# A Mamba scan taken in pairs of channel chunks, with the sum over states done by accumulating transposes

## Chip, cores and metric

One Trainium2 chip, one of its cores. The metric is the time of the whole kernel on the device in microseconds, the median of three runs. The kernel computes two transformer-like layers, and the change touches one helper that runs three times in it.

## The reference, cut to what matters

Each of the two layers adds an attention over a long context, a Mamba block and a feed-forward block to `x` (16 x 64 tokens of 512 channels). The Mamba blocks come down to a recurrence over the 64 tokens of each sequence, for each channel d and each of 16 states n:

```
xp = einsum('bld,rd->blr', x, x_proj_w)          # gives dt_in, B, C
dt = softplus(dt_in @ dt_proj_w + dt_proj_b)
dA = exp(dt[..., None] * A)                       # decay
dBx = dt[..., None] * B[:, :, None, :] * x[..., None]
h = dA_t * h + dBx_t                              # over tokens
y = einsum('bdn,bn->bd', h, C_t)                  # sum over the 16 states
y = y + D * x                                     # the skip
```

The block of layer 0 has 512 channels and adds `y` to `x`. The block of layer 1 has 1024 channels; there `y` is multiplied by a gate, `y * silu(gate)`, and then projected.

## The kernel before, in words

The kernel runs stage after stage; `Region.restart` and the end of each `nc.Block` are points at which all engines meet. The helper `scan_states` is called once in `l0_mamba` (tag `BS`, 4 chunks of 128 channels) and twice in `l1_mamba` (tags `ES0` and `ES1`, 4 chunks each). In the trace both calls of layer 1 bear the name `ES`.

Channels lie on the 128 partitions, and tokens along the free dimension: `HALF` is 512 tokens (8 sequences), there are two halves. A step is one (half, state n, chunk c): 2 x 16 x 4 = 128 steps in each call. A step goes through these engines:

- ScalarE makes the decay `dA` = exp(delta x A) for 504 of 512 tokens (L308; the first token of each sequence is kept at zero, so that one scan instruction serves 8 sequences), in a ring of `ND` = 3. It also makes the scaled input (L296): `duT` holds delta x u with tokens on partitions, and a piece is a [128 tokens, 512 channels] slice of it times the column B[:, n]. There are 4 pieces for each state and half, which serve 4 steps, so there is one piece per step.
- TensorE turns the pieces back to channels by tokens (`entering`, L401): 4 transposes of 128x128 fill one 512-wide buffer of `dB` in PSUM, ring `NE` = 3.
- VectorE runs the recurrence (`scan`, L357) on 512 tokens.
- The product with C (512 values broadcast to all partitions, loaded by SyncE's queue in `Rows.load_c`, ring of 4) is made on GpSimd (L330, `hcp`, ring `NP` = 4) in 7 of 8 steps, and on VectorE (L367, `hc`) in the eighth, where h stays in PSUM.
- TensorE adds the product to `acc` in PSUM (`add`, L417), as an fp32 matrix product of the identity with the [128, 512] product. The profile counts each such product as two instructions.
- After state 15 VectorE makes `out` = skip x D + acc (`finish`, L373). With a gate, the product with it is on GpSimd for the first half (L320) and on VectorE for the second (L377).

Each engine executes its own program in the written order and waits on semaphores; the loops are written out so that TensorE issues `entering` three steps ahead and `add` two to four steps behind. After the call `BS`, `l0_mamba` turns `yT` back with 32 transposes (L1371) and adds it to `X` on VectorE with 8 instructions (L1364), in a block of its own.

Of the kernel before, what the change touches and what calls it, by code (L numbers as in the profile page):

```python
# [8 lines left out]
ALU = mybir.AluOpType  # L9
# [3 lines left out]
P = 128  # L13
# [57 lines left out]
TOK = B * S  # L71
# [148 lines left out]
def c_on_pool(half, n, c):  # L220
    return c > 0 or n % 2 == 1


def scan_states(nc, consts, tag, delta, du, duT, b_col, A, rows, q0, CN, skip, skip_col, out, gate=None):

    with ExitStack() as stack:
        r = Region(nc, stack, tag)
        NH, NP, ND, NE = 2, 4, 3, 3
        TILES = HALF // P
        NB = len(B_ON_PE)  # L230
# [11 lines left out]
        hcp_ready = r.sem("hcp_ready")  # L242
        y_ready, gated = r.sem("y_ready"), r.sem("gated")
        STEPS = [(half, n, c) for half in range(2) for n in range(N_STATE) for c in range(CN)]
        LAST = {s: (half, c) for s, (half, n, c) in enumerate(STEPS) if n == N_STATE - 1}
        numbers = range(len(STEPS))
        on_dve = [s for s in numbers if not c_on_pool(*STEPS[s])]
        on_pool = [s for s in numbers if c_on_pool(*STEPS[s])]
        b_on_pe = [s for s in numbers if STEPS[s][2] in B_ON_PE]
        nth_dve = {s: k for k, s in enumerate(on_dve)}  # L250
        nth_pool = {s: k for k, s in enumerate(on_pool)}
        nth_pe = {s: k for k, s in enumerate(b_on_pe)}

        def decay(s):
            return dA[:, s % ND, :]

        def summed_at(s):

            return s + (2 if s in nth_dve else 4)

        sums = sorted(numbers, key=lambda s: (summed_at(s), s))
        nth_sum = {s: k for k, s in enumerate(sums)}

        def finished_at(s):

            return s + (4 if s in nth_dve else 7)

        finishes = sorted(LAST, key=lambda s: (finished_at(s), s))
        nth_finish = {s: k for k, s in enumerate(finishes)}

# [2787 lines left out]
```

## Time and profile before

| what | value |
| --- | --- |
| median of 3 runs | 3815.44 us (3812.68 to 3817.66) |
| profiled execution, from the first to the last instruction | 3813.4 us |
| difference of the two | 2.0 us |
| share of the span: PE, DVE, ACT, POOL | 94%, 60%, 41%, 34% |

PE is TensorE's matrix products and transposes, PEld its weight loads, DVE VectorE, ACT ScalarE, POOL GpSimd. A busy share over the whole span says little for this change: the three calls of the helper together take some 545 us of it, and only the rows of these stretches bear on them. The profile gives no separate time for the profiled execution beside its span; the sum of the prediction is made against the span and carried over to the median with the 2.0 us.

### The profile page before, as it was taken

Reading aid. Unit: us, or ns where it says so; the run is one execution under the profiler, and the core shown is the slowest. Engines: PE = TensorE matmul, PEld = TensorE weight load, DVE = VectorE, ACT = ScalarE, POOL = GpSimd, SP = SyncE. Lnnn points to the kernel's source line nnn. Section 1 sums busy time; section 2 is a strip of 40 time slices with the busy share of each in tenths; the row PEclk is TensorE's granted clock in tenths of the full one; section 3 lists DMA queues with packets and bytes.
Section 4 is the critical chain, followed back from the end, with each engine's and each line's share of the span. In section 5 each row is a group of like instructions: output and inputs, shape, how many; then the busy total and the mean of one; then the engine's idle time right before and its main releaser. Section 6 shows DMA issues by size and latency. Waiting matters only on the chain. (4 is left out here: it accounts for less than half of the span.)

```text
span 3813.4 us, 75996 instructions
## 1 busy us (share of the span) xinstructions
PE 3572.9 (94%) x32856; PEld 2539.3 (67%) x32856; DVE 2289.4 (60%) x2561; ACT 1578.1 (41%) x2153; POOL 1281.2 (34%) x792
## 2 busy tenths in 40 slices
PE   7999999999779679999999999999999998797998
PEld 4566666665245555888888888888888846454554
DVE  3677777777269842555555555555555416697972
ACT  2555555555179421222222222222222103697950
POOL 3344444442068321122222222222222004285861
PEclk8999999999779889999999999999999999898999
DMA  6455555553211032111111111111111112111110
GB/s 201 130 146 150 146 151 150 150 141 82 51 55 51 3 155 78 34 50 34 37 44 42 50 42 50 42 50 42 50 42 46 73 42 55 44 52 31 50 45 22
DMA packets 215252, 277.14 MB, mean 73 GB/s; under 512 B 67056, under 2 KB 165328, under 8 KB 213632
## 3 DMA queue, kind: packets, MB, share of 16 engines
q1 hardware_dynamic: 214920, 272.28, 24.6%
q8 instruction: 261, 4.28, 0.5%
q14 instruction: 71, 0.58, 0.1%
HBM read 218.63 MB, written 53.13 MB: 71 GB/s over the span
## 5 line engine op out<-in xcount | busy, mean ns | idle before, releaser
L1806 POOL TENSOR_TENSOR D_ctx_lo<-D_ctx_raw,D_ctx_hi 128x2048 fp32r<-128x2048 f32 (+1 forms) x64 | 269.6, 4213 | 1205.3 <-ACT D_ctx_hi L1800 1205.3
L748 DVE TENSOR_REDUCE A_mxc<-A_psX 128x2 f32<-128x768 f32 (+2 forms) x512 | 480.9, 984 | 113.8 <-PE A_psX L790 109.9
L1065 ACT ACTIVATE A_probs<-A_psE 128x1024 f32<-128x1024 f32 (+1 forms) x416 | 426.7, 1026 | 294.3 <-PE A_psE L1123 292.2
L1825 ACT ACTIVATE D_V<-D_psY 128x384 f32<-128x384 f32 x208 | 102.2, 491 | 890.2 <-PE D_psY L1891 890.2
L1841 DVE TENSOR_REDUCE D_mxc<-D_psE 128x4 f32<-128x1536 f32 (+2 forms) x128 | 241.9, 1890 | 204.2 <-PE D_psE L1919 204.2
L2182 ACT ACTIVATE D_probs<-D_psE 128x2048 f32<-128x2048 f32 x112 | 210.5, 1880 | 295.8 <-PE D_psE L2295 295.8
L330 POOL TENSOR_TENSOR ES_hcp<-E_du,E_Cn 128x512 f32<-128x512 f32 x224 | 285.3, 1278 | 128.3 <-DVE E_du L357 98.4
L2311 PE MATMUL D_psO<-D_probs,D_V 128*32 128x256 f32 (+1 forms) x5376 | 313.3, 381 | 0.0
L1891 PE MATMUL D_psY<-D_wv_hi,D_ctx_hi 128*128 128x384 f32 x832 | 285.5, 343 | 0.0
L1881 PE MATMUL D_psY<-D_ctx_hi,D_wk_hi 128*128 128x384 f32 (+2 forms) x768 | 279.8, 364 | 0.7 <-POOL D_ctx_lo L1806 0.7
L1891 PE MATMUL D_psY<-D_wv_hi,D_ctx_lo 128*128 128x384 f32 x832 | 279.1, 335 | 0.0
L1891 PE MATMUL D_psY<-D_wv_lo,D_ctx_hi 128*128 128x384 f32 x832 | 278.7, 335 | 0.0
L357 DVE TENSOR_TENSOR_SCAN E_du<-ES_dA,ES_dB 128x512 f32<-128x512 f32 x224 | 262.6, 1206 | 19.0 <-PE ES_dB L401 12.6
L1881 PE MATMUL D_psY<-D_ctx_hi,D_wk_lo 128*128 128x384 f32 (+2 forms) x768 | 268.3, 349 | 0.0
L1881 PE MATMUL D_psY<-D_ctx_lo,D_wk_hi 128*128 128x384 f32 (+2 forms) x768 | 268.2, 349 | 0.0
L2222 DVE TENSOR_TENSOR D_acc<-D_acc,D_probs 128x1024 f32<-128x1024 f32 x96 | 135.7, 1414 | 214.4 <-ACT D_probs L2182 212.9
L2311 PEld LDWEIGHTS D_psO<-D_probs,D_V 128*32 128x32 f32 (+1 forms) x5376 | 163.3, 110 | 115.8 <-issue 9.0
L1123 PEld LDWEIGHTS A_psE<-A_Qst,A_Kst 50*128 50x128 f32 (+1 forms) x1664 | 122.9, 184 | 172.1 <-ACT A_probs L1065 116.9
L1123 PE MATMUL A_psE<-A_Qst,A_Kst 50*128 50x256 f32 (+1 forms) x1664 | 211.2, 332 | 27.4 <-ACT A_probs L1065 19.3
L417 PE MATMUL ES_acc<-ES_hcp,all_ident 128*128 128x512 f32 x448 | 228.8, 597 | 0.0
L1138 PE MATMUL A_psO<-A_probs,A_V 128*17 128x256 f32 (+1 forms) x3328 | 228.5, 389 | 0.2 <-ACT A_probs L1065 0.2
L401 PEld LDWEIGHTS ES_dB<-all_ident,ES_scaled 128*128 128x128 f32 x1024 | 128.9, 145 | 132.9 <-issue 82.0
(372 smaller groups left out, 7864.0 us busy)
## 6 DMA issues: line engine op xcount, KB each, us to landing
A_land<-in_ctx SPq DMA_DIRECT2D x32, 768.0 KB, 5.7
D_ctx_raw<-in_ctx SPq DMA_DIRECT2D x32, 768.0 KB, 4.7
A_land<-in_ctx SPq DMA_DIRECT2D x16, 1024.0 KB, 6.0
D_ctx_raw<-in_ctx SPq DMA_DIRECT2D x16, 1024.0 KB, 5.9
E_Cn<-bc_scratch SPq DMA_DIRECT2D x64, 256.0 KB, 3.3
k_scratch<-A_Khl SPq DMA_DIRECT2D x32, 384.0 KB, 4.4
A_Kst<-k_scratch SPq DMA_DIRECT2D x64, 192.0 KB, 3.7
A_land<-in_ctx SPq DMA_DIRECT2D x16, 642.0 KB, 4.3
```

Of the source, the lines that this page charges most:

```text
L330: nc.gpsimd.tensor_tensor(hcp[:, k % NP, :], h_sb[:, k % NP, :], rows.C[:, q % NR, :], ALU.mult).then_inc(hcp_ready, 1)
L357: nc.vector.tensor_tensor_scan(to, decay(s), entering, 0.0, ALU.mult, ALU.add).then_inc(h_ready, 1)
L417: nc.tensor.matmul(acc[:, c, :], consts["ident"][:, :], product, start=(n == 0), stop=(n == N_STATE - 1)).then_inc(summed, 1)
L748: nc.vector.tensor_reduce(mxc[:, u % 4, :, u // 4], psX[:, x % 2, :, 0:w], axis=AX_X, op=ALU.max).then_inc(x_free, 1)
L1065: nc.scalar.activation(probs[0:KW[k], n % NPR, :, :].rearrange("p h q -> p (h q)"), psE[0:KW[k], :], ACT.Exp, scale=HD ** -0.5).then_inc(e ...
L1123: last = nc.tensor.matmul(psE[0:KW[k], col:col + HQ], Kst[j % 2][rows, 2 * g + pair, P * k:P * k + KW[k]], Qst[j % 2][rows, 2 * g + pair, ...
L1138: last = nc.tensor.matmul(psO[32 * h:32 * h + HD + 1, 0:HQ], V[j % 2][0:KW[k], k, HG * g + h, :], probs[0:KW[k], n % NPR, 2 * (h % 2) + h ...
L1806: nc.gpsimd.tensor_tensor(ctx_lo[c][:, :, 0:w], ctx_raw[c][:, :, 0:w], ctx_hi[c][:, :, 0:w].bitcast(F32), ALU.subtract).then_inc(lo_done[c ...
L1841: nc.vector.tensor_reduce(mxc[:, H * a:H * a + H, c], psE[:, :, 0:CH[c][1]], axis=AX_X, op=ALU.max).then_inc(x_free, 1)
L1881: last = nc.tensor.matmul(to[:, 0:w], wk_parts[a][:, d, bass.ts(t, P)], parts[a2][:, d, 0:w], start=(n == 0), stop=(n == len(PASSES) - 1))
L1891: last = nc.tensor.matmul(to[0:KWD[k], 0:H * HD], parts[a][:, d, at], wv_parts[a2][:, d, :], start=(n == 0), stop=(n == len(PASSES) - 1))
L2311: last = nc.tensor.matmul(psO[32 * h:32 * h + 32, t, :], V[0:KWD[k], k, h, bass.ts(t, 32)], probs[0:KWD[k], N % NPR, h, bass.ts(i, NQ)], s ...
```

## The change

`scan_states` is rewritten. A step now covers a pair of chunks (`W` = 2), so there are 64 steps in each call.

- The decay is still made by one instruction for each chunk, two in a step; all pieces of the scaled input are still on ScalarE, now two in a step, with a start order of its own (4 before the loop, 4, 3, 3 and 0 after steps 0 to 3).
- `entering` makes 8 transposes in a step into a pair-wide buffer, ring `NE` = 2. One scan instruction covers 1024 elements. One GpSimd instruction multiplies 1024 elements with C; VectorE takes no such product any more. `h` and `hc` lie in the memory of `du`, rings of 2.
- `add` no longer multiplies the identity with the product. It transposes the product block by block with `is_transpose` and accumulates in PSUM (8 transposes in a step), so that `acc` holds tokens on partitions. At state 15 the skip, which GpSimd has multiplied by D at the start of the call (4 instructions of 128x1024), is added by 8 more transposes.
- Without a gate (`BS`) VectorE adds `acc` straight to `X` (`finish`), and the block with 32 transposes and 8 additions after the call is gone. With a gate (`ES`) ScalarE copies `acc` to `yt` (`copy_out`, 8 instructions in a call), TensorE transposes it back into `acc` (`turn_back`), and VectorE multiplies with the gate.

The diff, cut (removed lines of the old loops stand in the functions above):

```diff
-def c_on_pool(half, n, c):
-    return c > 0 or n % 2 == 1
...
+def scan_states(nc, consts, tag, delta, du, duT, b_col, A, rows, q0, CN, skip, skip_col, finish_to, gate=None):
...
-        NH, NP, ND, NE = 2, 4, 3, 3
+        NH, NP, ND, NE, NS = 2, 2, 3, 2, 3
+        W = 2
+        CP = CN // W
         TILES = HALF // P
...
         acc = r.ps("acc", [P, CN, HALF])
-        dA = r.sb("dA", [P, ND, HALF])
-        h = r.ps("h", [P, HALF])
-        dB = r.ps("dB", [P, NE, HALF])
-        h_sb = du[:, 0:2, :].rearrange("p c (n t) -> p (c n) t", n=NP // 2)
-        scaled = r.sb("scaled", [P, 3, TILES, NB * P])
-        hc = r.sb("hc", [P, NH, HALF])
-        hcp = r.sb("hcp", [P, NP, HALF])
-        cleared, da_ready = r.sem("cleared"), r.sem("da_ready")
+        dB = r.ps("dB", [P, NE, W, HALF])
+        dA = r.sb("dA", [P, ND, W, HALF])
+        h = du[:, 0:2, :].rearrange("p k (w t) -> p k w t", w=W)
+        hc = du[:, 2:4, :].rearrange("p k (w t) -> p k w t", w=W)
+        scaled = r.sb("scaled", [P, NS, TILES, CN * P])
+        yt = r.sb("yt", [P, W, HALF]) if gate is not None else None
...
+        STEPS = [(half, n, cp) for half in range(2) for n in range(N_STATE) for cp in range(CP)]
+        LASTS = [s for s, (half, n, cp) in enumerate(STEPS) if n == N_STATE - 1]
+        nth_last = {s: k for k, s in enumerate(LASTS)}
+        PIECES = [(m, i) for m in range(2 * N_STATE) for i in range(TILES)]
+
+        def chunks(s):
+            return range(W * STEPS[s][2], W * STEPS[s][2] + W)
...
-                        sp.wait_ge(hc_ready, of_first(on_dve, k + 1))
-                        sp.wait_ge(hcp_ready, of_first(on_pool, k + 1))
+                        sp.wait_ge(hc_ready, CP * (k + 1))
...
-                    if m >= 3 and i == 0:
-                        act.wait_ge(db_full, NB * (m - 2))
-                    t = TILES * (m // N_STATE) + i
-                    nc.scalar.activation(scaled[:, m % 3, i, :], duT[:, t, :], ACT.Copy,
-                                         scale=b_col(t, m % N_STATE)).then_inc(scaled_ready, 1)
...
+                    if m >= NS and i == 0:
+                        act.wait_ge(db_full, CP * (m - NS + 1))
+                    to, of, col = piece(m, i)
+                    nc.scalar.activation(to, of, ACT.Copy, scale=col).then_inc(scaled_ready, 1)
+                def copy_out(s):
+                    k = nth_last[s]
+                    act.wait_ge(summed, s + 1)
+                    if k:
+                        act.wait_ge(turned, W * k)
+                    for j, c in enumerate(chunks(s)):
+                        nc.scalar.activation(yt[:, j, :], acc[:, c, :], ACT.Copy).then_inc(copied, 1)
                 ahead = 0
...
+                for p in PIECES[:TILES]:
+                    times_b(*p)
                     ahead += 1
                 act.wait_ge(cleared, 1)
...
+                for s, (half, n, cp) in enumerate(STEPS):
                     if s >= ND:
                         act.wait_ge(h_ready, s - ND + 1)
...
+                    for j, c in enumerate(chunks(s)):
+                        nc.scalar.activation(dA[:, s % ND, j, :].rearrange("p (b t) -> p b t", t=S)[:, :, 1:S],
+                                             tokens(delta, c, half).rearrange("p (b t) -> p b t", t=S)[:, :, 1:S],
+                                             ACT.Exp, scale=A[:, c, n:n + 1]).then_inc(da_ready, 1)
+                    for p in [p for p in PIECES[ahead:] if TILES * p[0] + p[1] < (2 * TILES, 11, 14, 8 + W * s)[min(s, 3)]]:
+                        times_b(*p)
                         ahead += 1
+                    if gate is not None and s - 3 in nth_last:
+                        copy_out(s - 3)
+                for s in LASTS:
+                    if gate is not None and s + 3 >= len(STEPS):
+                        copy_out(s)
             @block.gpsimd
             def _(pool):
...
+                for c in range(CN):
+                    nc.gpsimd.tensor_scalar(skip[:, c, :], skip[:, c, :], skip_col(c), None, ALU.mult
+                                            ).then_inc(skip_ready, 1)
+                for s, (half, n, cp) in enumerate(STEPS):
+                    q = ring_q(half, n)
                     pool.wait_ge(h_ready, s + 1)
...
+                    if s >= NP:
+                        pool.wait_ge(summed, s - NP + 1)
+                    if cp == 0:
+                        pool.wait_ge(rows.c_in[q % NR], 16 * (q // NR + 1))
+                    nc.gpsimd.tensor_tensor(hc[:, s % NP], h[:, s % NH],
+                                            rows.C[:, q % NR, :].unsqueeze(1).broadcast_to([P, W, HALF]), ALU.mult
+                                            ).then_inc(hc_ready, 1)
             @block.vector
             def _(dve):
...
+                nc.vector.memset(dA[:, :, :, :].rearrange("p k w (b t) -> p (k w) b t", t=S)[:, :, :, 0], 0.0
                                  ).then_inc(cleared, 1)
                 def scan(s):
...
+                    dve.wait_ge(da_ready, W * (s + 1))
+                    dve.wait_ge(db_full, s + 1)
+                    if s >= NH:
+                        dve.wait_ge(hc_ready, s - NH + 1)
+                    nc.vector.tensor_tensor_scan(h[:, s % NH].rearrange("p w t -> p (w t)"),
+                                                 dA[:, s % ND].rearrange("p w t -> p (w t)"),
+                                                 dB[:, s % NE].rearrange("p w t -> p (w t)"), 0.0,
                                                  ALU.mult, ALU.add).then_inc(h_ready, 1)
...
                 def finish(s):
...
+                    half = STEPS[s][0]
+                    for j, c in enumerate(chunks(s)):
+                        if gate is None:
+                            dve.wait_ge(summed, s + 1)
+                            at = finish_to[:, TILES * half:TILES * half + TILES, bass.ts(c, P)]
+                            nc.vector.tensor_tensor(at, acc[:, c, :].rearrange("p (i n) -> p i n", n=P), at, ALU.add
+                                                    ).then_inc(finished, 1)
+                        else:
+                            dve.wait_ge(turned, W * nth_last[s] + j + 1)
+                            nc.vector.tensor_tensor(tokens(finish_to, c, half), acc[:, c, :], tokens(gate, c, half),
+                                                    ALU.mult).then_inc(finished, 1)
+                for s in range(len(STEPS)):
                     scan(s)
...
+                    if s - 3 in nth_last:
+                        finish(s - 3)
+                for s in LASTS:
+                    if s + 3 >= len(STEPS):
+                        finish(s)
             @block.tensor
             def _(pe):
...
+                def entering(s):
+                    half, n, cp = STEPS[s]
+                    m = N_STATE * half + n
                     pe.wait_ge(scaled_ready, TILES * (m + 1))
...
+                    if s >= NE:
+                        pe.wait_ge(h_ready, s - NE + 1)
+                    for j, c in enumerate(chunks(s)):
+                        for i in range(TILES):
+                            last = nc.tensor.transpose(dB[:, s % NE, j, bass.ts(i, P)], scaled[:, m % NS, i, bass.ts(c, P)],
+                                                       consts["ident"][:, :])
                     last.then_inc(db_full, 1)
...
                 def add(s):
...
+                    half, n, cp = STEPS[s]
+                    pe.wait_ge(hc_ready, s + 1)
                     if half and n == 0:
...
+                        pe.wait_ge(finished, W * (nth_last[s - CP] + 1))
+                    for j, c in enumerate(chunks(s)):
+                        parts = [hc[:, s % NP, j, :]]
+                        if n == N_STATE - 1:
+                            pe.wait_ge(skip_ready, CN)
+                            parts.append(tokens(skip, c, half))
+                        for part in parts:
+                            for i in range(TILES):
+                                last = nc.tensor.matmul(acc[:, c, bass.ts(i, P)], part[:, bass.ts(i, P)],
+                                                        consts["ident"][:, :], start=(n == 0 and i == 0),
+                                                        stop=(n == N_STATE - 1), is_transpose=True,
+                                                        skip_group_check=True)
+                    last.then_inc(summed, 1)
+                def turn_back(s):
+                    for j, c in enumerate(chunks(s)):
+                        pe.wait_ge(copied, W * nth_last[s] + j + 1)
+                        for i in range(TILES):
+                            last = nc.tensor.transpose(acc[:, c, bass.ts(i, P)], yt[:, j, bass.ts(i, P)],
+                                                       consts["ident"][:, :])
+                        last.then_inc(turned, 1)
+                for s in range(NE):
+                    entering(s)
+                for s in range(len(STEPS) + 1):
+                    if s + NE < len(STEPS):
+                        entering(s + NE)
+                    if s:
+                        add(s - 1)
+                    if gate is not None and s - 2 in nth_last:
+                        turn_back(s - 2)
+                for s in LASTS:
+                    if gate is not None and s + 2 >= len(STEPS) + 1:
+                        turn_back(s)
...
-        t_full = r.sem("t_full")
...
-        yT = delta
-        scan_states(nc, consts, "BS", delta, du, duT, lambda t, n: Bt[:, t, R + n:R + n + 1], A, rows, 0, CN, XnT, lambda c: Dd[:, c:c + 1], yT)
-
-        acc = r.ps("acc", [P, CN, TOK])
-        with nc.Block() as block:
-            @block.vector
-            def _(dve):
-                for t in range(NPAIR):
-                    dve.wait_ge(t_full, t + 1)
-                    nc.vector.tensor_tensor(X[:, t, :], acc[:, t // 2, bass.ts(t % 2, 512)], X[:, t, :],
-                                            ALU.add)
-
-            @block.tensor
-            def _(pe):
-                for t in range(NPAIR):
-                    for c in range(CN):
-                        last = nc.tensor.transpose(acc[:, t // 2, 512 * (t % 2) + P * c:512 * (t % 2) + P * c + P],
-                                                   yT[:, c, bass.ts(t, P)], consts["ident"][:, :])
-                    last.then_inc(t_full, 1)
+        scan_states(nc, consts, "BS", delta, du, duT, lambda t, n: Bt[:, t, R + n:R + n + 1], A, rows, 0, CN, XnT,
+                    lambda c: Dd[:, c:c + 1], X)
...
                 scan_states(nc, consts, f"ES{g}", delta, du, duT, lambda t, n: pr[:, t, R + n:R + n + 1], A[:, chunk, :], rows, 2 * N_STATE * g, CG, U[:, chunk, :],
-                            lambda c: cols[:, CG * g + c, Dcol:Dcol + 1], U[:, chunk, :], Gt[:, chunk, :])
+                            lambda c: cols[:, CG * g + c, Dcol:Dcol + 1], U[:, chunk, :], gate=Gt[:, chunk, :])
```

## Rows read from the trace of the kernel before

**Rows 1.** A window of BS: PE, PEld, DVE, ACT, POOL busy; clock; DMA.

```profile
1175.00:1250.00 75.00, 74.79 (x345) 44.24 (x344) 71.55 (x69) 69.89 (x113) 64.02 (x51) 1.00 0.17 47
```

**Rows 2.** Timeline of BS, TensorE in steady steps: start, duration, engine, line, operation.

```profile
1175.05 1.02 PE L417 MATMUL BS_acc<-BS_hcp,all_ident 128*128 128x512 f32 x2
...
1175.91 0.60 PE L401 MATMUL BS_dB<-all_ident,BS_scaled 128*128 128x128 f32 x4
...
1176.35 1.02 PE L417 MATMUL BS_acc<-BS_hcp,all_ident 128*128 128x512 f32 x2
```

**Rows 3.** Timeline of BS, ScalarE in steady steps.

```profile
1095.64 0.70 ACT L308 ACTIVATE BS_dA<-B_delta,B_A 128x504 f32<-128x504 f32 x1
...
1102.95 0.70 ACT L308 ACTIVATE BS_dA<-B_delta,B_A 128x504 f32<-128x504 f32 x1
```

**Rows 4.** Groups by shape, POOL: count, busy us, mean ns, idle before.

```profile
L330 POOL TENSOR_TENSOR BS_hcp<-B_du,B_Cn 128x512 f32<-128x512 f32 x112 | 142.8, 1276 | 47.5 <-DVE B_du L357 27.1 <-PE BS_acc L417 18.8
...
L2610 POOL TENSOR_TENSOR E_U<-E_U,E_eu 128x1024 f32<-128x1024 f32 x7 | 23.9, 3418 | 32.3 <-ACT E_eu L2532 32.3
...
L1417 POOL TENSOR_TENSOR CW_gu<-CW_gu,CW_vec 128x1024 f32<-128x1024 f32 x2 | 4.7, 2344 | 12.4 <-DMA CW_vec<-in_L_ffn_vec 12.4
...
L1418 POOL CAST CW_gu_hi<-CW_gu 128x1024 fp32r<-128x1024 f32 x2 | 2.1, 1037 | 0.1
```

**Rows 5.** Timeline of BS, VectorE: runs of scans, and the additions after the call.

```profile
1250.99 4.54 DVE L357 TENSOR_TENSOR_SCAN B_du<-BS_dA,BS_dB 128x512 f32<-128x512 f32 x4
...
1265.45 4.87 DVE L1364 TENSOR_TENSOR all_X<-B_acc,all_X 128x512 f32<-128x512 f32 x8 [1.32 <-PE B_acc L1371]
```

**Rows 6.** Timeline, start of BS.

```profile
1085.85 2.56 ACT L296 ACTIVATE BS_scaled<-B_duT,B_Bt 128x512 f32<-128x512 f32 x4 [0.91 <-PEq L49]
...
1088.46 4.78 PE L401 MATMUL BS_dB<-all_ident,BS_scaled 128*128 128x128 f32 x20 [4.58 <-ACT BS_scaled L296]
...
1089.69 1.23 DVE L357 TENSOR_TENSOR_SCAN BS_h<-BS_dA,BS_dB 128x512 f32<-128x512 f32 x1 [3.69 <-PE BS_dB L401]
1090.88 1.22 DVE L357 TENSOR_TENSOR_SCAN B_du<-BS_dA,BS_dB 128x512 f32<-128x512 f32 x1
...
1092.18 1.28 POOL L330 TENSOR_TENSOR BS_hcp<-B_du,B_Cn 128x512 f32<-128x512 f32 x1 [20.41 <-DVE B_du L357]
```

**Rows 7.** Timeline, 8 transposes at the high and at the low clock.

```profile
3301.91 1.10 PE L2711 MATMUL E_z<-all_ident,E_du 128*128 128x128 f32 x8 [0.43 <-DVE E_du L2759]
...
3507.64 1.97 PE L2711 MATMUL E_z<-all_ident,E_du 128*128 128x128 f32 x8 [0.43 <-DVE E_du L2759]
```

**Rows 8.** Timeline, end of BS and what follows it.

```profile
1256.13 2.52 DVE L357 TENSOR_TENSOR_SCAN B_du<-BS_dA,BS_dB 128x512 f32<-128x512 f32 x2 [0.59 <-PE BS_dB L401]
...
1271.00 0.69 DVE L1460 BATCH_NORM_STATS2 C_stats<-all_X 128x6 f32<-128x512 f32 x1 [0.68 <-PEq L49]
```

**Rows 9.** Timeline, start and end of both ES calls; a copy from PSUM.

```profile
3304.69 1.95 ACT L296 ACTIVATE ES_scaled<-E_duT,E_pr 128x512 f32<-128x512 f32 x3 [0.62 <-PEq L49]
...
3484.91 0.69 DVE L377 TENSOR_TENSOR E_U<-E_U,E_Gt 128x512 f32<-128x512 f32 x1
...
3511.74 2.56 ACT L296 ACTIVATE ES_scaled<-E_duT,E_pr 128x512 f32<-128x512 f32 x4 [1.08 <-PEq L49]
...
3690.38 0.69 DVE L377 TENSOR_TENSOR E_U<-E_U,E_Gt 128x512 f32<-128x512 f32 x1
...
1282.05 0.60 ACT L1568 ACTIVATE C_qT<-C_psT 128x512 fp32r<-128x512 f32 x1 [3.64 <-PE C_psT L1610]
```

**Rows 10.** Windows of 1 us, start of BS; columns as rows 1.

```profile
1092.00:1093.00 1.00, 0.91 (x5) 0.72 (x4) 0.97 (x3) 1.00 (x3) 0.82 (x1) 0.50 0.00 0
1093.00:1094.00 1.00, 0.24 (x2) 0.00 (x0) 0.93 (x1) 1.00 (x3) 0.46 (x1) 0.99 0.00 0
...
1098.00:1099.00 1.00, 0.41 (x5) 0.20 (x4) 1.00 (x2) 1.00 (x3) 0.95 (x1) 1.00 0.62 133
...
1100.00:1101.00 1.00, 1.00 (x4) 0.48 (x3) 1.00 (x2) 1.00 (x2) 0.00 (x0) 0.50 0.01 2
```

More of the change, by code:

```diff
@@ L243, in scan_states @@
[L243 to L268, printed above, removed]
@@ L269, in scan_states @@
[L269 to L272 removed]
+        copied, turned, finished = r.sem("copied"), r.sem("turned"), r.sem("finished")
+        STEPS = [(half, n, cp) for half in range(2) for n in range(N_STATE) for cp in range(CP)]
+        LASTS = [s for s, (half, n, cp) in enumerate(STEPS) if n == N_STATE - 1]
+        nth_last = {s: k for k, s in enumerate(LASTS)}
+        PIECES = [(m, i) for m in range(2 * N_STATE) for i in range(TILES)]
@@ L333, in _ @@
-                for s, (half, n, c) in enumerate(STEPS):
-                    if s in nth_pool:
-                        times_c(s)
-                    if gate is not None and half and n in (3, 6, 9, 12) and c == CN - 1:
-                        gated_output(CN * (N_STATE - 1) + n // 3 - 1)
+                for c in range(CN):
+                    nc.gpsimd.tensor_scalar(skip[:, c, :], skip[:, c, :], skip_col(c), None, ALU.mult
+                                            ).then_inc(skip_ready, 1)
@@ L370, in finish @@
-                def finish(s):
-                    half, c = LAST[s]
-                    dve.wait_ge(summed, nth_sum[s] + 1)
-                    nc.vector.scalar_tensor_tensor(tokens(out, c, half), tokens(skip, c, half), skip_col(c),
-                                                   acc[:, c, :], ALU.mult, ALU.add).then_inc(y_ready, 1)
-                    if gate is not None and half:
-                        dve.wait_ge(y_ready, nth_finish[s] + 1)
-                        nc.vector.tensor_tensor(tokens(out, c, half), tokens(out, c, half), tokens(gate, c, half),
-                                                ALU.mult).then_inc(gated, 1)
@@ L403, in entering @@
                     last.then_inc(db_full, 1)
-                for k in range(NE):
-                    entering(k)
                 def add(s):
-                    half, n, c = STEPS[s]
-                    if s in nth_dve:
-                        pe.wait_ge(hc_ready, nth_dve[s] + 1)
-                        product = hc[:, nth_dve[s] % NH, :]
-                    else:
-                        pe.wait_ge(hcp_ready, nth_pool[s] + 1)
-                        product = hcp[:, nth_pool[s] % NP, :]
-                    if half and n == 0:
-                        pe.wait_ge(y_ready, nth_finish[s - CN] + 1)
-                    nc.tensor.matmul(acc[:, c, :], consts["ident"][:, :], product, start=(n == 0),
-                                     stop=(n == N_STATE - 1)).then_inc(summed, 1)
@@ L420, in _ @@
-                for s in range(len(STEPS) + 4):
-                    if s in nth_pe and nth_pe[s] + NE < len(b_on_pe):
-                        entering(nth_pe[s] + NE)
-                    for e in sums:
-                        if summed_at(e) == s:
-                            add(e)
+                    half, n, cp = STEPS[s]
+                    pe.wait_ge(hc_ready, s + 1)
+                    if half and n == 0:
+                        pe.wait_ge(finished, W * (nth_last[s - CP] + 1))
[10 more added lines that the diff above has]
+                                                        skip_group_check=True)
```

72 lines of the change are left out of this document (4 added, 68 removed).

## Prediction, made before the changed kernel ran

> **What bounds the kernel now.** The share of busy time of the whole page says only that TensorE is the busiest, so I went to the three stretches in which the helper runs. The windows of BS come first: in 75 us of its steady part TensorE is busy for 74.79, VectorE 71.55, ScalarE 69.89, GpSimd 64.02, at a clock of 1.00 [rows 1]. The timeline shows TensorE's rhythm: a group of 2 product instructions begins at 1175.05, 4 transposes follow at 1175.91, and the next products begin at 1176.35 [rows 2]. So a step of one chunk costs TensorE 1.30 us: 0.86 for the identity product in fp32 (2 x 0.43) and 0.44 for 4 transposes (0.11 each). Over the whole call a step takes little more: the first scan begins at 1089.69 and the last of 128 (the second of the group at 1256.13) at about 1257.4 [rows 6, 8], 167.7 / 127 = 1.32 us. TensorE is the bound, or 2.64 us for two chunks. The other limits lie close: ScalarE issues 12 instructions in 7.31 us, 0.609 each [rows 3], so two decays and two pieces take 2.44; two scans take 2 x 1.115 = 2.23 (four take 4.54, the last lasting 1.2) [rows 5]. A change that only frees TensorE can win 0.20 of 2.64 us before ScalarE stops it.
>
> **What the change costs, step by step.** X is the time of a pair step.
>
> TensorE: 8 `entering` and 8 accumulating transposes, 16 x 0.11 = 1.76 us where it had 2.60. No row shows a transpose that accumulates; the nearest is the plain fp32 transpose, 0.11, and the other end is the identity product, 0.43 x 2 / 4 = 0.21 for each block of 128. I take 0.11, since instruction form and operands are those of `entering`. By the other end TensorE would need 8 x 0.11 + 8 x 0.21 = 2.6 us.
>
> ScalarE: still 256 instructions in a call, 2.44 us a pair. Nothing of it goes away, and it is the new bound.
>
> VectorE: no row has a 1024-wide scan. Above, 2 x 1.115 = 2.23 us; below, 2.14, if the fixed 0.09 of one is saved. As recorded duration I take 1.20 + 1.07 = 2.27.
>
> GpSimd: all products now, at 1024 elements. Below: 2.34 us, the 128x1024 product of L1417; above: twice 1.276 = 2.55, and far above 3.42, the 128x1024 product of L2610, which ran beside VectorE instructions with two SBUF inputs [rows 4]. The scan has one input in PSUM, and the 112 products of BS beside it have a mean of 1.276, so I take 2.35.
>
> The rings are now only two pairs deep, which makes a loop: `scan`(s+2) waits for the product s, which waits for `scan`(s). A product starts 0.08 after its scan (1092.10 to 1092.18) [rows 6]. So 2X is at least 2.27 + 0.08 + 2.35 + 0.07 = 4.77, X 2.39. On TensorE `entering` waits for a scan, `add` is queued behind it, and the product after next waits for `add`: 0.1 + 16 x 0.11 + 0.3 = 2.2 us, inside X. Three limits within 0.1 us of each other (2.44, 2.39, 2.35) will not mesh perfectly; before, 1.32 came out where 1.30 was the bound (1.5%). I take X = 2.47, below 2.44, above 2.57 (products at 2.55).
>
> Start of a call: ScalarE makes 4 pieces, 2 decays, 4 pieces, 2 decays, 3, 2, 3, 2 before the decays of step 4, which end after 24 instructions at 24 x 0.61 + 0.1 = 14.8 us. Scan 3 waits until 13.6 for its decays and runs to 15.8, so scan 4 starts at 15.8. The first pair scan could start at 4.7 (8 slow transposes of 1.97 [rows 7] behind the first 2.56 us of pieces), so 2 us are lost against an even rhythm. The four skip products on GpSimd stand ahead of the first C product: between 4 x 1.04 (one input, L1418) and 4 x 2.34 us [rows 4], where the first scan ends at 6.9; at most 2.5 us late, of which some 0.7 reach scan 4. I take 0.3.
>
> The C loads stay as many, 32 rows in a call, one every two pair steps; SyncE's queue waits on one semaphore instead of two. GpSimd's idle time has no load among its causes now [rows 4], so I cost that at nothing; a row that came late would stop GpSimd and, through the loop, the scan.
>
> Middle (state 15 of the first half): in BS four additions go onto VectorE, 0.60 each [rows 5], between scans 33 and 35, and 16 more transposes into two `add`s. VectorE has 0.2 us of slack a pair, so 2 x 1.0 us is late, and much of it is regained against ScalarE's 2.44: 1.0 us. In ES ScalarE gets 4 copies of 0.60 [rows 9] there, 2.4 us on the bound itself, and the first decay waits behind them: 2.7 us.
>
> End: after scan 63 (2.27) come its product (0.08 + 2.35) and 16 transposes (0.11 + 1.10 + 8 x 0.11 = 2.1) [rows 7], 6.8 us in all. Then BS has two additions, 1.4. ES has `turn_back` of pair 62 queued first (0.9), two copies (1.3), 4 transposes for the last chunk (0.7) and one product (0.8): 3.7 us.
>
> **The sum.** BS at X = 2.44: 15.8 + 0.3 + 59 x 2.44 = 160.1; + 1.0 + 6.8 + 1.4 = 169.3, and 0.7 to the next stage [rows 8]: 170.0. Before: 1085.85 to 1271.00, 185.15 [rows 6, 8]. That is 15.1 less, of which the block of 32 transposes and 8 additions is 6.2 (4.87 for the additions and the 1.32 us that VectorE idles ahead of them [rows 5]). ES: 160.1 + 2.7 + 6.8 + 3.7 = 173.3, before 3304.69 to 3485.60 (180.9) and 3511.74 to 3691.07 (179.3) [rows 9]: 7.6 and 6.0 less. Together -28.7. X of 2.47 gives back 3 x 59 x 0.03 = 5.3: -23.4. The profiled execution's 3813.4 becomes 3790.0; with the 2.0 us between span and median, **3792 us**, 0.6% faster. In general the time is 3786.7 + 177 x (X - 2.44).
>
> **TensorE's clock, weighed.** In the start of BS TensorE does nothing but transposes from 1088.46 on (20 of them), and the granted clock goes from 0.50 (1.2 GHz) to 0.99 (2.4 GHz) at 1093; it is back at 0.50 at 1100, after windows like that of 1098, in which TensorE is busy for 0.41 [rows 6, 10]. Eight transposes take 1.97 us low and 1.10 high [rows 7]. The new loop has 16 transposes in 2.47 us, about 70% of the time at the high level. The Trainium skill, "TensorE: Matmul & The Clock Gate", Part 4, says that transposes do not count as busy and never get the full clock; rows 10 contradict the "never". By that rule TensorE would take 3.45 us a pair (rival A), and the sum would be 3965.
>
> **The rivals.**
>
> *A, the clock falls in the loop (slower).* The loop holds transposes alone. At the low level 8 transposes cost 1.97 - 1.10 = 0.87 us more [rows 7], a pair 1.71 + 2 x 0.87 = 3.45 us, and TensorE becomes the bound. For it: the fall at 1100. Against: at the low level the transposes fill TensorE, and that is the state in which the clock rose. Low all through: 3786.7 + 177 x 1.01 = 3965. Half of the time: X 2.95, 3877. It decides from X = 2.60, low in one sixth of the stretch. Chance 0.12, of which 0.02 for low all through, the case of the skill's rule.
>
> *B, GpSimd or the loop of two-deep rings is dearer (no change).* Products at 2.55, or accumulating transposes at 0.21 (2.6 us on TensorE), or the loop at more than its parts: X 2.55 to 2.65, 3806 to 3824. For it: no row has the 1024-wide product beside a scan, and a wait for two engines in turn is new. Against: 1024 elements cost 2.34 in L1417. Chance 0.20.
>
> *C, contention.* The product takes 3.4 us as in L2610: X 3.45, 3965. Against: the 112 of BS ran at 1.276 beside scans that kept VectorE 95% busy. Chance 0.03.
>
> *D, more is gained.* X at 2.44, nothing lost at start (3 x 2.3) nor in the middle (6.4): 3773. Chance 0.05.
>
> The forecast itself, X from 2.44 to 2.54, 3780 to 3804, has 0.60.
>
> **The numbers.** A measurement of this kernel tells about 0.2%, 7.6 us. Faster (under 3807.8): forecast, D, and a quarter of B: 0.70. Same: the rest of B up to 3823: 0.14. Slower: A, C and the last of B: 0.16. The range from 3776 to 3825 leaves out A, C and half of D.
>
> **What the next profile would show.** Right: in the loop ScalarE busy near 100%, its instructions 0.61 apart, scans of 128x1024 about 2.27 us and 2.47 apart, products about 2.35, TensorE some 0.11 a transpose at clock 1.00 with gaps between groups, no instruction between the last addition to `X` and the statistics of the next stage. Wrong: a clock under 0.9 in the windows of the loop (A); GpSimd without idle time and products of 2.5 or more (B, C); VectorE waiting for the products while ScalarE idles (the loop); a wait for C rows.

## The result and the profile after

The changed kernel takes 3792.61 us (median of 4 runs, 3789.08 to 3800.48); beside it the kernel before took 3814.69. The ratio is 0.9946, 95% interval 0.9933 to 0.9959: 0.5% faster. 3792 us was forecast. The total was met to 1 us, but partly by luck: the start of the calls was dearer than forecast, and a better pace and stretches outside the calls made up for it, as the stages show.

The windows of the steady part of BS and of an ES call, columns as in [rows 1]:

```profile
1112.00:1172.00 60.00, 47.25 (x391) 42.28 (x392) 56.40 (x26) 59.50 (x99) 57.99 (x26) 1.00 0.19 55
...
3320.00:3380.00 60.00, 48.07 (x399) 43.05 (x400) 56.39 (x25) 60.00 (x99) 58.03 (x25) 1.00 0.21 55
```

TensorE, busy in 99.7% of the window before [rows 1], has gaps now (79%), and its clock stays at 1.00 in these windows although some 390 transposes are all that it does in 60 us. ScalarE is busy for 59.5 to 60.0 of 60, GpSimd 58, VectorE 56.4. Read alone, this line says that ScalarE is the bound. The experiments show that it only keeps pace with a loop between two other engines.

The groups by shape (count, busy us, mean ns, idle before and its releasers), which answer to [rows 4, 5]:

```profile
L315 POOL TENSOR_TENSOR B_du<-B_du,B_Cn 128x1024 f32<-128x1024 f32 x64 | 150.9, 2372 | 7.7 <-DVE B_du L329 4.8 <-PE BS_acc L382 0.9 <-issue 0.6
L329 DVE TENSOR_TENSOR_SCAN B_du<-BS_dA,BS_dB 128x1024 f32<-128x1024 f32 x64 | 146.1, 2285 | 19.0 <-POOL B_du L315 11.8 <-PE BS_dB L365 4.5 <-ACT BS_dA L291 1.3
...
L291 ACT ACTIVATE BS_dA<-B_delta,B_A 128x504 f32<-128x504 f32 x128 | 83.9, 705 | 4.5 <-DVE B_du L329 4.5
...
L306 POOL TENSOR_SCALAR B_XnT<-B_XnT,B_Dd 128x1024 f32<-128x1024 f32 x4 | 11.3, 2846 | 17.6 <-POOLq L49 17.6
```

The product takes 2.37 us (2.35 forecast), the scan 2.285 (2.27). Most of VectorE's idle time ends with GpSimd's product, 11.8 of 19.0 us (4.07 of them at the start, below), and ScalarE's decays end only 1.3 of it. ScalarE itself waits 4.5 us for scans. The skip product by a column takes 2.85 us on GpSimd: above the upper end of its bounds, 2.34.

The timeline of the start of BS, against [rows 6]:

```profile
1088.64 2.56 ACT L272 ACTIVATE BS_scaled<-B_duT,B_Bt 128x512 f32<-128x512 f32 x4 [0.91 <-PEq L49]
1088.69 11.32 POOL L306 TENSOR_SCALAR B_XnT<-B_XnT,B_Dd 128x1024 f32<-128x1024 f32 x4 [17.62 <-POOLq L49]
...
1093.33 2.29 DVE L329 TENSOR_TENSOR_SCAN B_du<-BS_dA,BS_dB 128x1024 f32<-128x1024 f32 x1 [4.50 <-PE BS_dB L365]
...
1096.10 2.29 DVE L329 TENSOR_TENSOR_SCAN B_du<-BS_dA,BS_dB 128x1024 f32<-128x1024 f32 x1 [0.48 <-ACT BS_dA L291]
...
1099.97 4.68 POOL L315 TENSOR_TENSOR B_du<-B_du,B_Cn 128x1024 f32<-128x1024 f32 x2
...
1102.46 4.61 DVE L329 TENSOR_TENSOR_SCAN B_du<-BS_dA,BS_dB 128x1024 f32<-128x1024 f32 x2 [4.07 <-POOL B_du L315]
...
1107.33 2.29 DVE L329 TENSOR_TENSOR_SCAN B_du<-BS_dA,BS_dB 128x1024 f32<-128x1024 f32 x1 [0.26 <-POOL B_du L315]
```

The first scan is over at 1095.6, but GpSimd makes the skip until 1100.0. The third scan (1102.46) waits 4.07 us for the first product. With scans counted from 0, scan 4 (1107.33) begins 18.7 us after the call's first instruction, where 16.1 was forecast.

The ends of the calls, and what follows them (timeline; [rows 8, 9] before):

```profile
1260.61 1.29 DVE L340 TENSOR_TENSOR all_X<-BS_acc,all_X 128x512 f32<-128x512 f32 x2 [1.24 <-PE BS_acc L382]
1262.93 0.69 DVE L1424 BATCH_NORM_STATS2 C_stats<-all_X 128x6 f32<-128x512 f32 x1 [1.03 <-PEq L49]
...
3294.97 2.56 ACT L272 ACTIVATE ES_scaled<-E_duT,E_pr 128x512 f32<-128x512 f32 x4 [0.62 <-PEq L49]
...
3471.17 1.29 DVE L344 TENSOR_TENSOR E_U<-ES_acc,E_Gt 128x512 f32<-128x512 f32 x2 [0.55 <-PE ES_acc L392]
...
3496.75 2.56 ACT L272 ACTIVATE ES_scaled<-E_duT,E_pr 128x512 f32<-128x512 f32 x4 [0.62 <-PEq L49]
...
3672.73 1.29 DVE L344 TENSOR_TENSOR E_U<-ES_acc,E_Gt 128x512 f32<-128x512 f32 x2 [0.55 <-PE ES_acc L392]
3674.76 20.84 PE L2763 MATMUL E_acc<-E_wout,E_U 128*128 128x512 f32 x48 [1.57 <-PEq L49]
```

From these rows and those of before the 20.0 us between the two spans (3813.4 and 3793.4) fall into stages:

| stretch | before | after | difference | forecast |
| --- | --- | --- | --- | --- |
| start of the kernel to BS | 1085.85 | 1088.64 | +2.8 | 0 |
| BS to the next stage | 185.15 | 174.29 | -10.9 | -13.3 |
| next stage to ES0 | 2033.7 | 2032.0 | -1.7 | 0 |
| ES0 | 180.9 | 177.5 | -3.4 | -5.8 |
| between the calls | 26.1 | 24.3 | -1.9 | 0 |
| ES1 | 179.3 | 177.3 | -2.0 | -4.2 |
| ES1 to the end | 122.3 | 119.4 | -2.9 | 0 |

The forecast column is that of the prediction with its 5.3 us for X = 2.47 spread over the three calls. The calls gave 16.3 us instead of 23.4; stretches that the change does not touch gave 3.7 net. The first line is noise: in the profiled runs of this study BS begins between 1082.4 and 1091.6, with nothing changed ahead of it. The -1.7 stays unexplained: this stretch took 2033.0 to 2034.0 us in the three profiled runs with the old helper and 2030.6 to 2036.4 in the nine with the new one. The stretches between and after the ES calls are not noise, as shown below.

### The profile page after: what moved, and what is told of

Same layout as the page of the kernel before. It is cut to its first block and busy times, and to the rows that moved or that the text cites. A ratio compares the mean times of both kernels' runs of the same rounds, so it can differ in the third digit from the quotient of the medians.

```text
span 3793.4 us, 76745 instructions
## 1 busy us (share of the span) xinstructions
PE 3459.6 (91%) x33752; PEld 2592.3 (68%) x33752; DVE 2248.7 (59%) x2305; ACT 1579.7 (42%) x2169; POOL 1329.9 (35%) x652
## 3 DMA queue, kind: packets, MB, share of 16 engines
q1 hardware_dynamic: 214920, 272.28, 24.8%
## 5 line engine op out<-in xcount | busy, mean ns | idle before, releaser
L329 DVE TENSOR_TENSOR_SCAN E_du<-ES_dA,ES_dB 128x1024 f32<-128x1024 f32 x128 | 292.3, 2285 | 39.0 <-POOL E_du L315 23.5
L315 POOL TENSOR_TENSOR E_du<-E_du,E_Cn 128x1024 f32<-128x1024 f32 x128 | 301.7, 2373 | 19.2 <-DVE E_du L329 13.1
L2254 PE MATMUL D_psE<-D_Q_hi,D_K_hi 32*128 32x256 f32 (+1 forms) x2688 | 208.1, 294 | 5.7 <-PEq L49 5.7
L365 PE MATMUL ES_dB<-all_ident,ES_scaled 128*128 128x128 f32 x1024 | 143.0, 286 | 72.2 <-DVE E_du L329 63.6
```

The costliest lines, as they stand in the source:

```text
L315: nc.gpsimd.tensor_tensor(hc[:, s % NP], h[:, s % NH], rows.C[:, q % NR, :].unsqueeze(1).broadcast_to([P, W, HALF]), ALU.mult).then_inc(hc ...
L329: nc.vector.tensor_tensor_scan(h[:, s % NH].rearrange("p w t -> p (w t)"), dA[:, s % ND].rearrange("p w t -> p (w t)"), dB[:, s % NE].rear ...
```

## Experiments

Theory A, that of the prediction: ScalarE bounds the loop, and the start is what ScalarE's pieces make it. The rivals: the loop of scan and product over two-deep rings bounds (theory B); GpSimd's skip product holds the start; the transposes that accumulate are hidden and pairing alone is the gain. A further question: why stages after the calls got shorter. In what follows "scan 4" and "last scan" are times from the first instruction of the call, taken from the timeline.

### The skip product on VectorE

```diff
 gpsimd:
-    for c in range(CN):
-        nc.gpsimd.tensor_scalar(skip[:, c, :], skip[:, c, :], skip_col(c), None, ALU.mult).then_inc(skip_ready, 1)
 vector, after the memset of dA:
+    for c in range(CN):
+        nc.vector.tensor_scalar(skip[:, c, :], skip[:, c, :], skip_col(c), None, ALU.mult).then_inc(skip_ready, 1)
```

> The skip times D is made by VectorE (4 instructions of 128x1024 ahead of its first scan) instead of GpSimd. Theory (GpSimd's four products, 2.85 us each, hold the first C product and through the two-deep rings the third scan): VectorE does them in about 4 x 0.8 = 3.3 us, before the first scan can start at 4.7; scan 4 of each call begins 15.8 to 16.1 us after the call's first instruction instead of 18.7, each call is 2.6 us shorter, the kernel about 7.8 us faster than with the change, 0.9925 of the time before. Rival (the start is held by the order of ScalarE's pieces and by TensorE at the low clock): scan 4 stays at 18 or later, under 2 us in all.

Measured: 3784.23 us, 0.9922 of before (0.9907 to 0.9936), 8.4 us less than the change. The timeline of BS:

```profile
1090.85 0.73 DVE L321 TENSOR_SCALAR B_XnT<-B_XnT,B_Dd 128x1024 f32<-128x1024 f32 x1 [3.71 <-PEq L49]
...
1091.50 2.07 DVE L321 TENSOR_SCALAR B_XnT<-B_XnT,B_Dd 128x1024 f32<-128x1024 f32 x3
1095.47 2.29 DVE L329 TENSOR_TENSOR_SCAN B_du<-BS_dA,BS_dB 128x1024 f32<-128x1024 f32 x1 [1.90 <-PE BS_dB L365]
...
1106.96 4.61 DVE L329 TENSOR_TENSOR_SCAN B_du<-BS_dA,BS_dB 128x1024 f32<-128x1024 f32 x2 [0.33 <-POOL B_du L312]
```

The four products take 2.7 us on VectorE, in time in which it waited anyway. The first scan is no later (4.7 us) and scan 4 is at 16.2 instead of 18.7. The calls take 170.0, 173.4 and 173.3 us to their last result, where they took 173.3, 177.5 and 177.3. The late start was GpSimd's skip product. With it gone, the forecast's 16.1 for scan 4 holds to 0.1.

The calls are 3.2, 4.1 and 4.0 us shorter, more than the 2.6 expected. The rest can be read in the changed kernel's ES0, behind scan 4:

```profile
3310.00:3315.00 5.00, 4.46 (x22) 4.09 (x21) 4.71 (x3) 4.86 (x9) 3.34 (x2) 0.50 0.15 52
```

```profile
3312.94 1.91 PE L382 MATMUL ES_acc<-all_ident,E_du 128*128 128x128 f32 x8
...
3315.00 4.70 POOL L315 TENSOR_TENSOR E_du<-E_du,E_Cn 128x1024 f32<-128x1024 f32 x2 [1.49 <-PE ES_acc L382]
...
3317.52 4.59 DVE L329 TENSOR_TENSOR_SCAN E_du<-ES_dA,ES_dB 128x1024 f32<-128x1024 f32 x2 [1.60 <-POOL E_du L315]
```

The clock is still at 0.50, 8 transposes take 1.9 us instead of 1.04, the product waits 1.49 us for them, and a scan waits for the product. In the changed kernel the granted clock goes up for good some 18 us (BS) and 20 us (ES) after a call's first instruction, with the skip product on VectorE after 13.3 to 14.5 us. While GpSimd made the skip, TensorE had little to do (1.93 us of idleness before its first sum).

### Half of ScalarE's piece work, and deeper rings

```diff
-    nc.scalar.activation(to, of, ACT.Copy, scale=col).then_inc(scaled_ready, 1)
+    nc.scalar.activation(to[:, 0:256], of[:, 0:256], ACT.Copy, scale=col).then_inc(scaled_ready, 1)
```

> Each scaled piece is made for 256 of its 512 columns (the other half is left as it lies in memory), so ScalarE needs about 1.9 us for a pair step where it needed 2.44. Theory A (ScalarE alone is the bound of the loop at 2.44; the loop of scan and product over two-deep rings is at 2.40): steady scans 2.39 to 2.41 us apart, 2 to 3 us less in each call. Theory B (the loop of rings is as dear as ScalarE): they stay at 2.43 to 2.44, and no call gets shorter by 1 us in its steady part.

Measured: 3797.49 us in one run, 3795.8 in the profiled span. The pace did not move: BS's scans are 2.435 us apart between scans 6 and 30, as with full pieces. The timeline of BS:

```profile
1142.10 4.62 DVE L329 TENSOR_TENSOR_SCAN B_du<-BS_dA,BS_dB 128x1024 f32<-128x1024 f32 x2 [0.25 <-POOL B_du L315]
...
1144.43 1.32 ACT L291 ACTIVATE BS_dA<-B_delta,B_A 128x504 f32<-128x504 f32 x2 [0.41 <-DVE B_du L329]
1144.47 4.70 POOL L315 TENSOR_TENSOR B_du<-B_du,B_Cn 128x1024 f32<-128x1024 f32 x2 [0.16 <-DVE B_du L329]
...
1146.97 4.61 DVE L329 TENSOR_TENSOR_SCAN B_du<-BS_dA,BS_dB 128x1024 f32<-128x1024 f32 x2 [0.25 <-POOL B_du L315]
```

ScalarE waits now for the scans, and the loop can be read off: a scan of 2.29 us from 1142.10, 0.08 to the product at 1144.47, its 2.37 to 1146.84, 0.13 to the scan two steps on at 1146.97. That is 4.87 us for two steps, 2.435 each. Theory A falls: ScalarE's 2.437 is as large by coincidence, and the loop sets the pace too.

The rings of `h` and `hc` three deep in BS (8 KB more on each partition; the ES calls keep two):

```diff
-        NH, NP, ND, NE, NS = 2, 2, 3, 2, 3
+        NH, NP, ND, NE, NS = 2 if gate is not None else 3, 2 if gate is not None else 3, 3, 2, 3
...
+        if gate is None:
+            more = r.sb("more", [P, 2, W * HALF])
+            hbuf.append(more[:, 0, :])
+            cbuf.append(more[:, 1, :])
```

Together with the half pieces:

> As the run with half pieces, and in the call of layer 0 the rings of h and of its product with C are three pairs deep instead of two (the calls of layer 1 keep two). Theory A: with ScalarE and the ring loop both out of the way the call of layer 0 runs at GpSimd's own pace, 2.37 us a pair, 2 us shorter than with half pieces alone. Theory B (the waits between scan and product are not what holds it): no difference between the two runs in that call.

Measured: 3787.10 us in one run. BS takes 164.7 us to its last addition, 8.5 less than with half pieces alone (173.1), and its scans are 2.28 us apart. Four times what was expected, although its end got longer (11.2 us from the last scan instead of 8.1, with the clock at 0.50 for a part of it; the last experiment below has the same). The window:

```profile
1120.00:1170.00 50.00, 42.09 (x344) 36.87 (x343) 49.27 (x23) 46.23 (x88) 50.00 (x23) 1.00 0.20 59
```

GpSimd has no gap left. Its products, 2.38 us as recorded, follow each other every 2.28, so back to back they overlap by 0.1 us, and 2.37 was too dear as a bound of GpSimd. And the deep rings alone:

> The changed kernel with rings of h and of the C product three deep in the call of layer 0. If ScalarE bounds the loop, steady scans stay 2.44 us apart and only the middle (1.9 us late) and the start get shorter, by 1 to 3 us in this call. If the ring loop bounds it, the pace goes to 2.40 or less.

Measured: 3788.45 us in one run. BS 166.6 instead of 173.3, its scans 2.35 apart up to scan 30 and 2.39 behind scan 38; the last scan begins at 158.2. Both theories had a part: the loop alone held the pace at 2.435, and with the loop out of the way ScalarE's 256 instructions are the bound. ScalarE is never idle now and ends its last decay after 156.2 us; in the changed kernel it had to wait for scans and ended at 161.4.

### The sum by products again, in the ES calls

```diff
+                        if gate is not None:
+                            for k, part in enumerate(parts):
+                                last = nc.tensor.matmul(acc[:, c, :], consts["ident"][:, :], part,
+                                                        start=(n == 0), stop=(n == N_STATE - 1 and k == 1))
+                            continue
...
-    calls of copy_out and turn_back
```

> In the two calls of layer 1 the sum over states is again made by products with the identity (fp32, 128x512), with no copy and no turning back; pairs, rings and everything else stay. Theory (TensorE then needs 8 x 0.107 + 4 x 0.43 = 2.57 us a pair and is the bound again): steady scans 2.58 to 2.62 us apart, TensorE without gaps, some 9 us more in the loop of each call and 3 to 5 us less in the middle and at the end: each call about 181 to 183 us where it was 177.4, the kernel 8 to 11 us slower than with the change. Rival (pairing alone gave the gain, the kind of sum is hidden): steady scans stay 2.44 apart and the calls get 3 us shorter.

Measured: 3817.19 us, 1.0006 of before (0.9997 to 1.0016), 24.6 us more than the change. Each ES call takes 189.2 and 189.1 us to its last result, some 11.8 more, and scans are 2.62 to 2.63 us apart. The window and the timeline of ES0:

```profile
3330.00:3380.00 50.00, 49.88 (x230) 28.78 (x229) 43.44 (x20) 48.31 (x77) 44.87 (x20) 1.00 0.19 53
```

```profile
3342.18 1.06 PE L360 MATMUL ES_dB<-all_ident,ES_scaled 128*128 128x128 f32 x8
...
3343.08 1.88 PE L377 MATMUL ES_acc<-E_du,all_ident 128*128 128x512 f32 x4
...
3344.80 1.05 PE L360 MATMUL ES_dB<-all_ident,ES_scaled 128*128 128x128 f32 x8
```

TensorE is full: 8 transposes (0.90) and 4 product instructions (1.72) make 2.62. The theory's mechanism holds, its size does not: 7 us a call were missing, since the pace is 0.19 above the change's (59 x 0.19 = 11) and nothing was gained back at the end. Pairing without the transposed sum makes the ES calls 8 to 10 us slower than before the change (180.9 and 179.3). So there is no gain without the transposed sum. What pairing adds to it is not shown: no run has the transposed sum in steps of one chunk.

### The clock behind the calls

In the kernel before, TensorE has nothing to do from its last sum to the next stage, while VectorE finishes; then 48 product instructions take 23.60 us, after the change 20.84. The windows in which they begin, before and after (the column behind GpSimd's is the clock):

```profile
3691.00:3700.00 9.00, 8.17 (x13) 3.66 (x14) 0.07 (x1) 0.00 (x0) 0.00 (x0) 0.64 0.58 206
```

```profile
3674.00:3680.00 6.00, 5.24 (x13) 2.40 (x14) 0.02 (x1) 0.00 (x0) 0.00 (x0) 1.00 0.71 247
```

To keep TensorE at work there, in the kernel before:

```diff
+                if gate is not None:
+                    pe.wait_ge(h_ready, len(STEPS))
+                    for k in range(40):
+                        nc.tensor.transpose(dB[:, 0, bass.ts(k % TILES, P)], consts["ident"][:, :],
+                                            consts["ident"][:, :])
```

> The kernel before, with 40 transposes of the identity into an unused buffer after TensorE's last sum of each call of layer 1 (nobody reads them), so that TensorE is not idle while VectorE finishes. Theory (the stages after the calls got shorter because TensorE's clock was still at the high level when they began): the stretch from the last product with the gate to the end of the kernel goes from 122.3 to about 119.5 us, the stretch between the two calls from 26.1 to about 24.5, the kernel 3 to 5 us faster than before. Rival (these stretches got shorter by something else, such as where the data lies): they stay at 122.3 and 26.1.

Measured: 3813.10 us, 0.9996 (0.9987 to 1.0006), inconclusive in the total; the 3 to 5 us expected did not come. From the last product with the gate to the end it was 120.8 us (3694.68 to 3815.5), but between the calls 26.2 as before. The 40 transposes end at 3695.6, 1 us behind VectorE, and hold the next stage up. Between the calls the next stage's 8 products take 2.10 us where they took 3.41, but begin 0.9 us later. So with 26:

> The kernel before with 26 instead of 40 transposes of the identity behind the last sum of the two calls of layer 1, so that they end with VectorE's last product and don't hold up the next stage. Theory (high clock at the start of the next stage): the first 48 product instructions after the second call take 20.8 us instead of 23.6, from the last product with the gate to the end of the kernel it is 119.5 us instead of 122.3. Rival: the work behind the calls is not shorter than 122.

Measured: 3811.18 us in one run. The timelines of TensorE, before and with 26 transposes:

```profile
3691.83 23.60 PE L2799 MATMUL E_acc<-E_wout,E_U 128*128 128x512 f32 x48 [4.16 <-PEq L49]
```

```profile
3686.38 3.00 PE L429 MATMUL ES_dB<-all_ident 128*128 128x128 f32 x26
3690.70 20.84 PE L2804 MATMUL E_acc<-E_wout,E_U 128*128 128x512 f32 x48 [1.31 <-PEq L49]
```

From the last product (3689.94) to the end of the span (3809.5) it is 119.6 us, where it was 122.3: the 2.8 us of the 48 products. Between the calls it is 24.8 us, where it was 26.1. The change has 119.4 and 24.3; there `turn_back` gives TensorE work until 1.6 us before the next stage. That alone is no guarantee: with the skip product on VectorE the pause is 1.57 us as well, but the clock fell to 0.50 just there, the 48 products take 22.38 us and the stretch 120.3.

### ScalarE's start order, and what beats both kernels

Pieces two after every step from the first on, on top of the skip product on VectorE:

```diff
-  if TILES * p[0] + p[1] < (2 * TILES, 11, 14, 8 + W * s)[min(s, 3)]
+  if TILES * p[0] + p[1] < 6 + W * s
```

> Skip product on VectorE as in the first run, and ScalarE's pieces issued two after every step from the first on (4 ahead of the loop), so fewer pieces stand before the first decays. Theory (pieces issued ahead cost start time): scan 4 begins at about 14.5 us instead of 16, each call 1.3 us shorter than with the skip product moved alone, 4 us in all. Rival (pieces then come just in time, and TensorE hands its buffer over late in every second step): steady scans 2.5 us or more apart, slower than with the skip product moved alone.

Measured: 3778.77 us, 0.9912 (0.9898 to 0.9925). Scan 4 begins at 14.9, 14.4 and 15.0 us, and the calls end 1.2, 1.0 and 1.1 us earlier than with the skip product moved alone. The pace is unharmed in BS (2.436) and 0.02 worse in ES0.

The ring of `h` alone three deep, in all calls (4 KB more), with the skip product on VectorE and the change's own order of pieces:

```diff
-        NH, NP, ND, NE, NS = 2, 2, 3, 2, 3
+        NH, NP, ND, NE, NS = 3, 2, 3, 2, 3
...
+        more = r.sb("more", [P, W * HALF])
+        h = [du[:, 0, :], du[:, 1, :], more[:, :]]
```

> Skip product on VectorE, and the ring of h alone three pairs deep in all three calls (the ring of its product with C stays two deep). Theory (the wait of the scan for the product two steps back sets 2.435; without it ScalarE's 2.437 less what it is ahead at the start bounds): in the call of layer 0 the last scan begins at 157 to 158.5 us after the call's first instruction and the call ends at 165.5 to 167 instead of 170.0; the calls of layer 1, with 2.4 us of copies on ScalarE, end at 170 to 171.5 instead of 173.3; the kernel 8 to 10 us faster than with the skip product moved alone. Rival (the product's own wait, for the sum two steps back, is as tight): pace stays 2.435 and nothing is gained.

Measured: **3774.96 us, 0.9891 of before (0.9876 to 0.9907)**, the best of all, 17.7 us less than the change. The calls end at 166.6, 170.9 and 170.9, inside the ranges expected. ScalarE is idle in none of them up to its last decay. The window of BS:

```profile
1110.00:1170.00 60.00, 48.20 (x400) 43.23 (x400) 56.47 (x26) 60.00 (x100) 59.06 (x26) 1.00 0.21 56
```

And both together:

> The same with ScalarE's pieces two after every step from the first on. If ScalarE bounds the loop, its order at the start no longer matters much, since it has the same 256 instructions before the last scan: within 1 us of the run before in each call. If the start still counts, 1 us less in each call as it was with two-deep rings.

Measured: 3776.80 us, 0.9901 (0.9887 to 0.9915), not to be told from the run before it. The last scans begin 0.3 to 1.0 us earlier, but the calls end 0.8 to 1.5 later, at 167.4, 172.4 and 172.5. The second was not expected. It is the clock. The last sums of BS, first in the run before, then in this one, with a window of this one:

```profile
1248.60 0.66 PE L383 MATMUL BS_acc<-all_ident,B_du 128*128 128x128 f32 x4 [1.22 <-POOL B_du L313]
```

```profile
1245.05 1.07 PE L383 MATMUL BS_acc<-all_ident,B_du 128*128 128x128 f32 x4 [1.22 <-POOL B_du L313]
```

```profile
1246.00:1247.00 1.00, 1.00 (x7) 1.00 (x6) 0.00 (x0) 0.00 (x0) 1.00 (x1) 0.50 0.00 0
```

In all three calls of this run the granted clock falls to 0.50 for 3.4 us behind the last scan, and 4 transposes take 1.07 us instead of 0.60 to 0.66; in the run before it stays at 1.00 there. Before it fell TensorE had paused for 0.81 us (BS) and, one sum later, for 1.22; in the run before the same pauses are 0.41 and 1.22. Whether this difference decides it is not shown.

## Why the prediction was right, and where it was not

**The removed bound.** Right. TensorE's 16 transposes cost what plain ones cost (8 in 1.04 to 1.06 us, 0.11 each): a transpose that accumulates is no dearer here, and the other end of that bound (0.21) did not come about.

**The price of a pair step.** X = 2.47 was forecast, 2.435 to 2.45 came. But the reason given, ScalarE as the new bound with the ring loop just below it at 2.39, was only half of a tie. The loop's parts were each a little low: 2.285 + 0.08 + 2.37 + 0.13 = 4.87, where the sum had 2.27 + 0.08 + 2.35 + 0.07 = 4.77. Half of ScalarE's piece work taken away changed nothing; with a third buffer of `h` the calls got 2.3 to 3.5 us shorter. The ring loop stood among the three limits and in rival B as a danger; it held the pace all along, without being a loss against X.

**The start.** The step that failed. "Between 4 x 1.04 and 4 x 2.34 us" for the skip products, "of which some 0.7 reach scan 4", costed at 0.3: they took 4 x 2.85 and 2.6 us more than forecast reached scan 4. The bounds were taken from a cast and from a product of two tensors; no row of GpSimd's product with a column was at hand, and it was dearer than both. The prediction also let TensorE be slow only for the first 8 transposes, but with the late start the clock rose for good only after 18 to 20 us, and another 1.3 to 1.4 us went in each ES call, 0.5 in BS, between scans 4 and 30. The run with the skip product on VectorE gives the whole price: 3.2, 4.1 and 4.0 us, 11.3 in the three calls.

**Middle and end.** The middle costs 1.9 us in BS (scans 30 to 37 take 19.04 us, seven steps of 2.44 are 17.1), 1.0 forecast, and 3.2 in ES, 2.7 forecast. Nothing of it was regained: scans behind the middle stay 2.44 to 2.45 apart. From the last scan to the last result 8.1 us in BS (8.2 forecast) and 10.3 in ES (10.5).

**The sum.** The calls gave 16.3 us, 23.4 were forecast. The start took 11.3 of them away and the middle and the ends 1.5; the pace, 2.44 instead of 2.47, gave 5.3 back. That makes 16. With the skip product on VectorE the calls take 170.0, 173.4 and 173.3 us, where the prediction's terms at X = 2.44 had 169.3, 173.3 and 173.3: the start was the one term that was far off. The total came closer than the calls' 7 us only through what the prediction did not have: the stretches between and behind the ES calls gave 1.9 and 2.9 us through the clock (1.4 and 2.8 of them were got with 26 dummy transposes), the stretch between BS and ES0 gave 1.7 from a cause not found, and 2.8 went by variation ahead of BS. The profiled spans differ by 20.0 us, where 23.4 were forecast; that the medians meet to 1 us is luck.

**The rivals.** A did not happen as told: behind the first 18 to 20 us of a call the clock stays at 1.00 through the loop, at 79% busy, with transposes alone. Its mechanism was there in the start, as above. The Trainium skill, "TensorE: Matmul & The Clock Gate", Part 4, has it that transposes do not engage the full clock (it tells so of a bf16 transpose in one kernel; the "never" is the prediction's). Here fp32 transposes hold it at 1.00 for over 150 us in each of three calls, and the measurement decides. B, at X 2.55 or more, and C, contention at 3.4 us, did not happen. D wanted nothing lost at the start nor in the middle, and both were lost.

## What to carry to other kernels

When an edit frees the busiest engine, write down every ring that closes a loop between two engines, add its parts with both handovers (0.08 and 0.13 us here), and compare it with the busiest engine left; a busy share of 100% on one engine does not show that it is the bound, since it may only just keep pace with the loop. One buffer more in the right ring (4 KB) and a one-time product moved to an engine that was waiting were worth 17.7 us here, nearly as much as the whole rewrite. And account by stages: a total that fits can hide terms that cancel.

## What was not expected of the hardware

GpSimd's `tensor_scalar` with a column takes 2.85 us for 128x1024 in fp32, more than its `tensor_tensor` of the same size (2.34 to 2.37); VectorE does it in 0.73. GpSimd's products recorded at 2.38 us follow each other every 2.28. And what TensorE did in the last microseconds of one stage set the speed of the next: 48 product instructions took 23.60 us after 4.2 us of idleness and 20.84 after transposes on the identity.
